# A fused decoder layer on one core: the feed-forward's normalising, range and quantisation moved up between the softmax maxima, with its root first on POOL and its transposes ahead of the mixing product

## The reference

```
x = x + mamba(layernorm(x))                # in-projection, causal convolution of 4 taps, SiLU,
                                           # state-space mixing in chunks of 64, gate, RMS norm, out-projection
x = x + cross_attention(layernorm(x), ctx) # 16 query heads on 4 key/value heads of 128, RMS-normed q and k,
                                           # softmax(q k^T / sqrt(128) + mask) v, out-projection
x = x + ffn(layernorm(x))                  # 8-bit activations, ternary weights:
    s  = 127 / max(|x|, 1e-5)              # one scale for each token
    qx = clip(round(x * s), -128, 127) / s
    h  = silu(qx @ Wg) * (qx @ Wu);  h = rms_norm(h) * w;  out = quantised(h) @ Wd
```

## Time and profile before

| | |
|---|---|
| runs | 1315.02, 1319.17, 1319.58 us; median 1319.17 us |
| profiled execution: own time | 1314.49 us |
| profiled execution: span of its instructions | 1312.6 us, mean granted TensorE clock 0.979 |
| busy: PE, PEld, DVE | 1227.9 us (94%), 1026.8 us (78%), 1041.2 us (79%) |
| busy: ACT, POOL | 691.1 us (53%), 797.0 us (61%) |
| chain that ended last | PE 88%, DVE 4%, POOL 3%, issue 2%, ACT 2%, DMA 1% |

### The profile page before, as it was taken

The page is one execution under the profiler, slowest core; times in us unless marked ns, Lnnn a source line. Parts: engine busy times, 40 slices in busy tenths (PEclk is TensorE's granted clock), DMA queues, the critical chain, the costliest instruction groups (busy, mean ns, idle before and its releaser), DMA issues.

```text
span 1312.6 us, 32089 instructions
## 1 busy us (share of the span) xinstructions
PE 1227.9 (94%) x10775; PEld 1026.8 (78%) x10807; DVE 1041.2 (79%) x2582; ACT 691.1 (53%) x1579; POOL 797.0 (61%) x1434
## 2 busy tenths in 40 slices
PE   3579999999999999999999999999999999999965
PEld 3467788888888888888888888888888888888743
DVE  3666788888888888888888888888888888888555
ACT  1345555455665555556655455665555556555432
POOL 2445567766666676666667765666676666657541
PEclk9689999999999999999999999999999999999987
DMA  7400000000000000000000000000000000000000
GB/s 232 143 10 12 14 14 17 17 12 12 12 16 16 12 16 16 8 12 16 16 12 16 16 16 8 12 16 16 12 16 16 12 8 16 12 13 13 6 4 8
DMA packets 30373, 28.62 MB, mean 22 GB/s; under 512 B 7680, under 2 KB 28672, under 8 KB 30080
## 3 DMA queue, kind: packets, MB, share of 16 engines
q1 hardware_dynamic: 27984, 24.99, 6.2%
q10 hardware_dynamic: 2352, 3.15, 0.7%
HBM read 23.93 MB, written 4.19 MB: 21 GB/s over the span
## 4 chain that ended last, share of the span: by engine, by line
PE 88%; DVE 4%; POOL 3%; issue 2%; ACT 2%; DMA 1%; SPq 0%; POOLq 0%; DVEq 0%; ACTq 0%
PE bank L1270 17%; PE bank L1360 16%; PE bank L1352 5%; PE bank L1330 5%; PE bank L1193 4%; PE bank L1202 4%; PE bank L1243 4%; PE bank L1165 3%; PE bank L1233 2%; PE bank L1385 2%; PE bank L1283 2%; PE bank L1182 2%; PE bank L1380 2%; PE bank L1166 2%; PE bank L1167 2%; PE bank L1340 2%
## 5 line engine op out<-in xcount | busy, mean ns | idle before, releaser
L1270 PE MATMUL bank<-xcT,wq 128*128 128x128 f32 x2048 | 237.9, 277 | 2.5 <-ACT xcT L620 2.5
L1270 PEld LDWEIGHTS bank<-xcT,wq 128*128 128x128 f32 x2048 | 232.7, 193 | 7.3 <-issue 3.1
L1360 PE MATMUL bank<-wo,oT 128*128 128x256 f32 x1024 | 231.4, 379 | 0.0
L1360 PEld LDWEIGHTS bank<-wo,oT 128*128 128x128 f32 x1024 | 189.9, 190 | 23.5
L830 DVE SCALAR_TENSOR_TENSOR xc<-bank,cw,xc 128x124 f32<-128x124 f32 (+2 forms) x576 | 163.9, 340 | 9.2 <-ACT xc L590 2.0
L635 ACT ACTIVATE qT<-bank,bqT 128x128 f32<-128x128 f32 x384 | 109.5, 368 | 51.5 <-PE bank L1270 51.2
L358 POOL TENSOR_SCALAR m_mv<-m_mv 128x1 f32<-128x1 f32 x32 | 6.9, 215 | 157.2 <-DVE m_mv L798 157.1
L426 POOL TENSOR_TENSOR rq<-rq,minus_half 128x16 f32<-128x16 f32 x32 | 93.1, 2909 | 7.8 <-DVE rq L928 7.8
L984 DVE SCALAR_TENSOR_TENSOR h<-h,bank 128x512 f32<-128x512 f32 x64 | 44.0, 688 | 63.4 <-ACT h L674 63.4
L438 POOL TENSOR_TENSOR pr<-pr,mask 128x512 f32<-128x512 f32 x64 | 83.0, 1316 | 15.0 <-DVE pr L935 15.0
L448 POOL TENSOR_TENSOR pr<-pr,mx 128x512 f32<-128x512 f32 x64 | 65.5, 1043 | 40.8 <-DVE mx L947 40.8
(11 more groups left out here) (221 smaller groups left out, 3047.8 us busy)
## 6 DMA issues: line engine op xcount, KB each, us to landing
x_in<-in_x SPq DMA_DIRECT2D x32, 128.0 KB, 2.0
c_in<-in_ctx SPq DMA_DIRECT2D x32, 128.0 KB, 2.0
x_m<-in_x SPq DMA_DIRECT2D x32, 128.0 KB, 2.0
out<-x SPq DMA_DIRECT2D x32, 128.0 KB, 1.7
wq<-in_L_xattn_Wq SPq DMA_DIRECT2D x1, 2048.0 KB, 9.4
wo<-in_L_xattn_Wo SPq DMA_DIRECT2D x1, 2048.0 KB, 12.3
w_in<-in_L_attn_W_in SPq DMA_DIRECT2D x1, 1288.0 KB, 8.5
qT<-in_L_ffn_w_gate ACTq DMA_DIRECT2D x1, 1024.0 KB, 9.2
```

What stands on the lines that cost most here:

```text
L1270: last = mm(x_Qbank[g][:, (n % 4) * P:(n % 4 + 1) * P], wq[:, c, n * HD:(n + 1) * HD], xcT[:, c, :], start=(c == 0), stop=(c == DC - 1))
L1360: last = mm(X1[:, 0:D], oT[:, n, :, :], wo[:, n, :], start=(n == 0), stop=(n == NH - 1))
```

## The change

Calls change their place in four queues; no instruction is added or removed in a pass.

```
@@ POOL body
             def body(ms, mn, m, xa, xb, f, fb, first=None):
-                if m is not None:
-                    m_decay_in(m)
+                if f is not None:
+                    f_norm(f)
                 if xa is not None:
                     x_norm(xa)
                 if xb is not None:
...
                     x_mask(xb, 1)
                     x_sub(xb, 0)
                     x_sub(xb, 1)
-                if f is not None:
-                    f_norm(f)
-                if xa is not None:
-                    x_split(xa)
+                if m is not None:
+                    m_decay_in(m)
                 if xb is not None:
                     x_prob(xb, 0)
                     x_prob(xb, 1)
+                if xa is not None:
+                    x_split(xa)
@@ ACT body
                 if xb is not None:
                     x_o_copy(xb, 0, 0)
                     x_o_copy(xb, 0, 1)
+                if f is not None:
+                    f_T_copy(f)
                 if xa is not None:
                     x_q_square(xa, 3)
                 if xb is not None:
                     x_o_copy(xb, 1, 0)
                     x_o_copy(xb, 1, 1)
-                if f is not None:
-                    f_T_copy(f)
@@ DVE body
+                if f is not None:
+                    f_norm(f)
+                    f_range(f)
                 if xb is not None:
                     x_max(xb, 0)
+                if f is not None:
+                    f_quant(f)
                 if xb is not None:
                     x_max(xb, 1)
...
-                if f is not None:
-                    f_norm(f)
-                    f_range(f)
                 if m is not None:
                     m_xdt(m)
                     m_mix(m)
-                if f is not None:
-                    f_quant(f)
@@ PE body
-                if m is not None:
-                    m_mix(m, mn)
                 if f is not None:
                     f_transpose(f)
+                if m is not None:
+                    m_mix(m, mn)
```

More of the change, by code:

```diff
@@ L1457, in body @@
                     x_attend(xb, 1, xa)
+                if f is not None:
+                    f_transpose(f)
                 if m is not None:
                     m_mix(m, mn)
-                if f is not None:
-                    f_transpose(f)
                 if first == 1:
```

## The result

| | before | changed |
|---|---|---|
| median of the runs | 1319.17 us | 1361.89 us (1360.15 to 1362.13) |
| profiled execution, span | 1314.49, 1312.6 us | 1360.15, 1358.3 us |
| ratio | | 1.0329, 95% interval 1.0313 to 1.0345 |

The forecast was 1367 us within 1342 to 1385.

A forecast was written before the change was run, and what follows sets the result against it. PE's queue was taken as the bound. Later DVE inputs cost 1.8 us a pass, the lost wait gave back 0.2; 1.6 in 29 passes is 46, with the ends 48, so 1319.17 becomes 1367 us, range 1342 to 1385.

The forecast's parts named there:

- The bound and the slack: PE's queue sets the pass; POOL's second multiplication and DVE's L847 reach PE with only 0.05 to 0.2 us slack.
- The meeting of DVE's wide instructions with POOL's: Moved f_xn and L978 wait for whole POOL instructions under the masks and first subtraction, delaying the second maximum 1.8 us a pass.
- The narrow instructions: One-column DVE instructions of the range, such as L967, don't wait for POOL and keep their 0.15 us.
- the rival of 1384: Narrow DVE instructions wait for POOL too: L967 waits for the second mask, 2.2 us a pass, 1384 us; chance 0.07.
- The grant between two queued POOL instructions: A waiting wide DVE instruction goes between the running POOL instruction and the next, which gives way for 0.05 us only.
- The gapless rival: POOL runs its pairs without a gap, so f_xn ends only behind the second mask: 2.8 us a pass, 1402; chance 0.04.
- The roundings slip in: Rival: the first subtraction waits for both roundings, 0.9 us net a pass, 1346; 1356 if f_xn also precedes a mask; chance 0.2.
- The wait ahead of the mixing product: PE's wait for DVE ahead of L1233 goes, through PE's new order and less DVE work ahead: -0.2 us a pass.
- The ends: Last passes: nothing for pass 32, up to +1.8 us for pass 33, at the most -0.4 for the last pass.
- The level: The forecast median was the profiled execution's 1362 us plus the 4.7 by which the median of before stood above its execution.

The follow-up runs named there:

- run 1: The changed kernel with its three wide feed-forward tensor_scalar instructions (L789 on f_xn, L976, L978) also writing an unused sum: 1327.3 us, ratio 1.0071 to the kernel before.
- run 4: The changed kernel with its PE and ACT parts undone, so the mixing product is ahead of the feed-forward's transposes: 1357.74 us, ratio 1.0307 to the kernel before.
- run 6: The kernel before with POOL's roots first and m_decay_in behind the subtractions, x_split left ahead of the last multiplications: 1314.01 us, ratio 0.9972.
- run 3: The kernel before with the change's POOL part and, on DVE, only f_norm and f_range moved ahead of the first maximum: 1318.74 us, ratio 1.0014.
- run 2: The changed kernel with f_quant behind both maxima instead of between them: 1393.6 us, ratio 1.0581 to the kernel before.

## Why the prediction was right, and where it was off

- **The bound and the slack.** Right: PE's queue set the pass, and DVE's lateness of 1.74 us at the second maximum reached L1224 as 1.73. The slack of 0.05 to 0.2 that the prediction saw took nothing that could be told. The gap on PE opens one step earlier than it said, though: the first four transposes of L1340 wait for DVE's L921 (620.83 + 0.67 = 621.50), which stands between the sums and L847, and not for POOL's first multiplication, over at about 621.25. The second four and L1224 then wait for POOL's second multiplication (until 622.25) and L847 (until 622.80), as forecast.
- **The meeting of DVE's wide instructions with POOL's.** Right, and shown by run 1. f_xn 1.36 us (predicted 1.36), L978 1.01 (1.01 to 1.02), 1.74 in all (1.8).
- **The narrow instructions.** Right: L967 took 0.15 under the second mask. The section of the Trainium skill that the prediction set against the row says that a tensor_scalar can take both ports, on conditions that it leaves to another page; read without an exception for one column, it doesn't hold for this instruction here, and the rival of 1384 falls.
- **The grant between two queued POOL instructions.** Right: L789 got in between the masks, and the second mask gave way for 0.05 (1.32 against 1.27). The gapless rival falls.
- **The roundings slip in.** Fell: the subtraction was issued under L976 (613.77) and was running when L978 came (613.99).
- **The wait ahead of the mixing product.** It went, by DVE's part alone (run 4, whose pass is 39.27 - 37.79 = 1.48 above before, so 1.73 - 0.25; its mixing product starts 3.08 us behind L1224, before 3.33). The prediction put it at 0.2, from the 0.18 of PE's list of waits. The failed step is the order on PE: the transposes ahead of the mixing product, which the prediction took as free, cost 0.14. The changed kernel's pass is 1.73 - 0.25 + 0.14 = 1.62 above before; that the prediction said 1.6 is in part two small errors of opposite sign.
- **The filling.** Not foreseen: x_norm's root ahead of m_decay_in in pass 1. The scores of pass 2 start 2.0 us earlier than before (98.23 against 100.20); how much of it is the order is told under run 6. The prediction treats m_decay_in in the steady pass alone, where POOL's root of x isn't held up.
- **The ends.** From the starts of the scores in both traces, passes 2 to 30 gained 45.3 us in length, pass 31 1.2, pass 32 nothing, pass 33 with the last one 1.2; less 2.0 of filling this is the 45.7 us by which the spans differ. Predicted were 46 for passes 3 to 31, where it was 46.5, nothing for 32, and up to 1.4 for the end, where it was 1.2.
- **The level.** 1367 stood on the difference of 4.7 us between the profiled execution and the median of before. In the changed kernel that difference is 1.7 (1361.89 against 1360.15). The increase itself was 48 predicted, 45.7 measured on the profiled executions.

## What to carry to other kernels

Idle time of VectorE that is a wait for GpSimd is no free slot for a wide tensor_scalar from SBUF to SBUF: GpSimd is running in just that time, and the instruction waits for its end. Such a wait costs what the idle time doesn't cover, little for f_norm and f_range in run 3, much once f_quant follows. What ran there at its usual length were reductions, one-column instructions and, in run 1, the form that also writes a sum. Cost a moved instruction by what runs on the other engine at its new place, and follow the delay to the next thing the bound engine takes in without slack. When waits move between engines, undo the parts one by one: here the DVE part cost all, the POOL part held a gain of its own, and a split in which the moved instructions meet nothing of GpSimd came out 0.6% below the kernel before.

## What the runs showed of the hardware that I had not expected

- TensorE's granted clock can fall after a single gap in an otherwise full pass. With PE's gap ahead of L1340 of 1.3 us at L1340 (1.7 on the weight loads) it stayed at 1.00 in all passes of the changed kernel's steady stretch; with 1.7 (2.1 on the weight loads) it fell in eleven of the passes of run 2, in the one shown to 0.69 over 4.3 us behind the gap, and such a pass was 1.53 us longer. Why some passes and not others is open.
- Behind two bfloat16 transposes the mixing product started 0.22 us later, the key product 0.07: the order of three small groups on PE was worth 0.14 us a pass.
